# Turning the input by DMA and projecting it as float16 pieces, in an attention and expert kernel

## The reference

```
q  = (xn @ Wq.T + bq) * D**-0.5        # 256 columns: 16 heads of D = 16
kv = xn @ Wkv.T + bkv                  # 32 columns: one key and one value head for all 16
a  = softmax(q_heads @ k.T) @ v        # per batch 16*512 query rows against 512 keys
attn = a @ Wo.T + bo
logits = xn @ w_gate                   # 6 experts, the best one is taken
attn_e = softmax(xn @ tokens_e.T / 16) # 100 tokens for each expert, of rank 16
delta  = ((attn_e @ val_e + xn) @ wd.T + wd_b) * scale
out = x + attn + xn + log(exp(delta of the chosen expert))
```

## Time and profile before

| | |
|---|---|
| median of 3 runs | 976.48 us (974.66 to 976.85) |
| span of the profiled execution | 972.5 us; the median of the runs is 3.98 us above this span, the time around it |
| PE busy | 907.7 us, 93% of the span |
| DVE busy | 808.2 us, 83% |
| ACT busy | 682.1 us, 70% |
| POOL busy | 459.1 us, 47% |
| DMA engines | 29.9% on the one hardware queue |
| mean granted PE clock | 0.981 |

### The profile page before, as it was taken

One profiled execution on the slowest core, in us unless ns is written; L12 is line 12 of the kernel. 1 busy time (PEld: TensorE's weight loads), 2 busy tenths in 40 slices (PEclk: granted clock), 3 DMA queues, 4 the chain that ended last, 5 costly groups with the idle time before them and its releaser, 6 DMA issues.

```text
span 972.5 us, 17720 instructions
## 1 busy us (share of the span) xinstructions
PE 907.7 (93%) x5868; PEld 354.1 (36%) x5868; DVE 808.2 (83%) x1556; ACT 682.1 (70%) x1380; POOL 459.1 (47%) x567
## 2 busy tenths in 40 slices
PE   4889999999999999999999999999999999998976
PEld 3433333333434333343334333333333334332323
DVE  5688978889898888989888898989889898888814
ACT  1217777877777777777777777777777777777791
POOL 3654545554554555455444655444465544524200
PEclk9779999999999999999999999999999999999998
DMA  4230232422324242422423242242423223241120
GB/s 118 70 59 31 76 67 71 91 87 81 91 72 100 63 98 79 95 76 83 88 84 79 89 91 69 91 82 93 88 71 91 81 76 84 71 90 46 58 66 33
DMA packets 86192, 76.07 MB, mean 78 GB/s; under 512 B 18263, under 2 KB 70232, under 8 KB 86104
## 3 DMA queue, kind: packets, MB, share of 16 engines
q1 hardware_dynamic: 86104, 74.94, 29.9%
HBM read 39.28 MB, written 33.54 MB: 75 GB/s over the span
## 4 chain that ended last, share of the span: by engine, by line
PE 75%; DVE 6%; DMA 6%; ACT 6%; POOL 3%; issue 2%; SPq 2%; POOLq 0%; DVEq 0%
PE pO L349 22%; PE pA L331 14%; PE pB L336 8%; PE pA L470 6%; PE pA L412 6%; PE pA L488 5%; DVE M L750 3%; DMA o_parts<-OTr 3%; ACT P L597 3%; PE pA L472 3%; PE pA L402 3%; PE pB L392 2%; SPq L937 2%; PE pA L443 2%; DMA Rb<-l_parts 2%
## 5 line engine op out<-in xcount | busy, mean ns | idle before, releaser
L750 DVE TENSOR_REDUCE M<-pA 128x1 f32<-128x512 f32 x1024 | 652.4, 680 | 82.7 <-PE pA L331 80.9
L597 ACT ACTIVATE P<-pB 128x512 f32<-128x512 f32 x1002 | 553.5, 599 | 147.6 <-PE pB L336 143.1
L331 PE MATMUL pA<-K,Q 48*128 48x512 f16 x1024 | 316.8, 387 | 19.9 <-DVE M L750 10.3
L336 PE MATMUL pB<-Q,K 50*128 50x512 f16 x1002 | 307.3, 383 | 0.3 <-ACT P L597 0.3
L349 PE MATMUL pO<-P,VK 128*32 128x512 f32 x2048 | 272.8, 605 | 11.1 <-ACT P L597 7.9
L331 PEld LDWEIGHTS pA<-K,Q 48*128 48x128 f16 x1024 | 64.0, 94 | 323.2 <-DVE M L750 243.8
L887 POOL TENSOR_TENSOR On<-Op,Rb 128x512 f32<-128x512 f32 x31 | 39.9, 1288 | 146.9 <-DMA Rb<-l_parts 104.7
L873 POOL TENSOR_SCALAR Cz<-Cx 128x512 f32<-128x512 f32 x32 | 62.0, 1936 | 50.4 <-ACT Cx L579 50.4
L349 PEld LDWEIGHTS pO<-P,VK 128*32 128x32 f32 x2048 | 40.4, 108 | 108.3 <-issue 82.2
L412 PE MATMUL pA<-xT,wq 128*128 128x256 f32 x256 | 74.1, 416 | 1.3 <-ACT xT L541 0.7
L488 PE MATMUL pA<-wo,On 128*128 128x256 f32 x248 | 69.9, 407 | 4.3 <-DVE RL L763 2.5
(11 more groups left out here) (130 smaller groups left out, 865.7 us busy)
## 6 DMA issues: line engine op xcount, KB each, us to landing
o_parts<-OTr SPq DMA_DIRECT2D x62, 256.0 KB, 2.3
Q<-q_pieces SPq DMA_DIRECT2D x90, 128.0 KB, 4.1
X<-in_x SPq DMA_DIRECT2D x16, 512.0 KB, 3.9
q_pieces<-Qp SPq DMA_DIRECT2D x32, 256.0 KB, 2.1
out<-OUT SPq DMA_DIRECT2D x32, 256.0 KB, 3.1
Op<-o_parts SPq DMA_DIRECT2D x31, 256.0 KB
Rb<-l_parts SPq DMA_DIRECT2D x31, 256.0 KB
K<-KS SPq DMA_DIRECT2D x96, 16.0 KB, 1.8
```

The costliest lines, as they stand in the source:

```text
L331: e.matmul(bank1("ab", t)[:, :], Q16[r:r + 48, b % 2, h, 128 * s:128 * s + 128], K16[r:r + 48, b % 3, :], start=True, stop=True).then_inc( ...
L336: e.matmul(bankB(t)[:, :], K16[r:r + 50, b % 3, 128 * i:128 * i + 128], Q16[r:r + 50, b % 2, :, 32 * hh:32 * hh + 32], start=True, stop=Tr ...
L597: e.activation(P[:, u % PR, :], bankB(u + LB)[:, :], ACT.Exp, scale=alpha).then_inc(S("e"))
L750: e.tensor_reduce(M[:, t // 32 % 2, t % 2, t % 32 // 2:t % 32 // 2 + 1], bank1("ab", t)[:, :], AX, ALU.max, negate=True).then_inc(S("mx"))
```

## The change

`XN` is now scaled by 2^10 and split into two float16 pieces `XP` (`pieces`: POOL a cast and a subtraction; for batch 0 ACT and DVE do it in two halves). SP turns both pieces by one DMA transpose per batch (`xtd`; two for batch 0) into `xT`, now float16. The weights are scaled and split once at the start (`wqP`, `wcP`), and each projection is three float16 products (`PIECES`), over 512 tokens at a time for q and uk, with the scale taken out where the result is evicted. The mask is turned by a DMA transpose too (`mkd`). `Rs` starts from `X` alone (four `tensor_scalar` of 256 columns in place of one `tensor_tensor` of 1024), so `XN` needs one buffer. Slots move.

```diff
+PIECES = ((0, 0), (0, 1), (1, 0))
+XS = 2.0 ** 10
 SLOT = {
-    "root": -91.4, "refine": -90.2, "norm": -87.2, "xt0": -73.1, "xte0": -72.4, "xt1": -69.1, "xte1": -68.4,
-    "residual": 2.3, "q00": -57, "qe00": -56.4, "q01": -53, "qe01": -52.4, "qs0": -51.2, "qw0": -48.2,
+    "root": -91.4, "refine": -90.2, "norm": -87.2, "pieces": -84.2, "xtd": -74.2,
+    "residual": 2.3, "q0": -57, "qe0": -55.4, "qs0": -53.8, "qw0": -50.2, "uk": -53, "uke": -51.4, "ks": -50.2,
...
-                for c in range(2):
-                    if (b := due(f"xt{c}", n)) is not None:
...
-                            mm = e.transpose(bank2(f"xt{c}", b)[:, 128 * i:128 * i + 128],
-                                             XN[:, b % 2, i, 128 * c:128 * c + 128], idf[:, :])
...
+                for g in range(2):
+                    if (b := due(f"q{g}", n)) is not None:
+                        w.wait_ge(*before1(f"q{g}", b))
+                        w.wait_ge(S(f"xt_{b % 2}"), turned(b))
+                        w.wait_ge(S("wqp"), 2)
+                        for k, (wp, xp) in enumerate(PIECES):
+                            for c in range(2):
+                                mm = e.matmul(bank1(f"q{g}", b)[:, :], wqP[:, wp, c, 128 * g:128 * g + 128],
+                                              xT[:, b % 2, :, xp, c, :], start=(k == 0 and c == 0), stop=(k == 2 and c == 1))
                         mm.then_inc(S(f"q{g}"))
...
-                        for c in range(2):
-                            e.matmul(dst, xT[:, b % 2, c, 128 * t:128 * t + 128], wc[:, c, 0:C],
-                                     start=(c == 0), stop=False)
+                        for k, (wp, xp) in enumerate(PIECES):
+                            for c in range(2):
+                                e.matmul(dst, xT[:, b % 2, t, xp, c, :], wcP[:, wp, c, 0:C],
+                                         start=(k == 0 and c == 0), stop=False)
...
-                    o = bank2("mk", b)[:, :].bitcast(BF16)
-                    for i in range(4):
-                        mm = e.transpose(o[0:ER, 128 * i:128 * i + 128], mk[:, i, :], idb[:, :])
...
+                if (b := due("pieces", n)):
+                    w.wait_ge(S("xn"), 4 * b + 4)
+                    w.wait_ge(S(f"xt_{(b - 1) % 2}"), turned(b - 1))
+                    e.tensor_copy(XP[:, :, 0, :], XN[:, :, :]).then_inc(S("xh"))
+                    w.wait_ge(S("xh"), b)
+                    e.tensor_tensor(XP[:, :, 1, :], XN[:, :, :], XP[:, :, 0, :], ALU.subtract).then_inc(S("xl"))
...
                 if (b := due("utm", n)) is not None:
-                    w.wait_ge(S("mke"), b + 1)
+                    w.wait_ge(S("mkd"), 16 * (b + 1))
...
+                if (b := due("xtd", n)) is not None:
+                    w.wait_ge(S("d"), 4 * (b - 1))
+                    if b:
+                        w.wait_ge(S("xl"), b)
+                    for i0, i1 in ((0, 2), (2, 4)) if b == 0 else ((0, 4),):
+                        if b == 0:
+                            w.wait_ge(S("xl0"), i1 // 2)
+                        e.dma_start_transpose(xT[:, b % 2, i0:i1].rearrange("p i k c t -> p (i k c) t"),
+                                              XP[:, i0:i1].rearrange("p i k n -> p (i k n)")).then_inc(S(f"xt_{b % 2}"), 16)
+
+                if (b := due("mkd", n)) is not None:
+                    w.wait_ge(S("mk"), b + 1)
+                    w.wait_ge(S("mk1"), 1)
+                    w.wait_ge(S("mm"), b)
+                    w.wait_ge(S("utm"), b)
+                    e.dma_start_transpose(mkT[:, :].rearrange("p (i t) -> p i t", t=128),
+                                          mk[:, :, :].rearrange("p i n -> p (i n)")).then_inc(S("mkd"), 16)
```

More of the change, by code:

```diff
@@ L306, in before2, with turned @@
             return FREED2[TURNS[1][k][1]](TURNS[1][k][2]) if k >= 0 else (S("id"), 0)
+        def turned(b):
+            return 16 * (b // 2 + 1) + 16 * (b % 2 == 0)
         block = ctx.enter_context(nc.Block())
@@ L362, in _ @@
                     w.wait_ge(*before1("bs", 0))
-                    w.wait_ge(S("ones"), 5)
+                    w.wait_ge(S("ones"), 4)
                     w.wait_ge(S("two"), 1)
-                    e.matmul(bank1("bs", 0)[:, 0:3], one[:, :], fac[:, 0:3], start=True, stop=True).then_inc(S("bs"))
+                    e.matmul(bank1("bs", 0)[:, 0:7], one[:, :], fac[:, 0:7], start=True, stop=True).then_inc(S("bs"))
                 for h in range(2):
@@ L396, in _ @@
-                for k in range(2):
-                    if (b := due(f"uk{k}", n)) is not None:
-                        w.wait_ge(*before1(f"uk{k}", b))
-                        w.wait_ge(S("xte"), 2 * b + 2)
-                        w.wait_ge(S("wcs"), 1)
-                        for c in range(2):
-                            mm = e.matmul(bank1(f"uk{k}", b)[0:UKW, 0:C], wc[:, c, U0:U0 + UKW],
-                                          xT[:, b % 2, c, C * k:C * k + C], start=(c == 0), stop=(c == 1))
-                        mm.then_inc(S("uk"))
@@ L417, in _ @@
                     w.wait_ge(*before2("vg", b))
-                    w.wait_ge(S("xte"), 2 * b + 2)
-                    for c in range(2):
-                        for i in range(4):
-                            mm = e.matmul(bank2("vg", b)[32 * i:32 * i + 32, 0:128], wc[:, c, V0:V0 + 32],
-                                          xT[:, b % 2, c, 128 * i:128 * i + 128], start=(c == 0), stop=(c == 1))
+                    w.wait_ge(S(f"xt_{b % 2}"), turned(b))
+                    w.wait_ge(S("wcp"), 2)
+                    for k, (wp, xp) in enumerate(PIECES):
+                        for c in range(2):
+                            for i in range(4):
+                                mm = e.matmul(bank2("vg", b)[32 * i:32 * i + 32, 0:128], wcP[:, wp, c, V0:V0 + 32],
+                                              xT[:, b % 2, i, xp, c, :], start=(k == 0 and c == 0), stop=(k == 2 and c == 1))
                     mm.then_inc(S("vg"))
@@ L534, in _ @@
                     w.wait_ge(S("w2"), 1)
-                    e.copy(W2[0:ER + 1, :], bank2("w2", 0)[0:ER + 1, 0:C]).then_inc(S("w2e"))
-                for c in range(2):
-                    if (b := due(f"xte{c}", n)) is not None:
-                        w.wait_ge(S("xt"), 2 * b + c + 1)
-                        w.wait_ge(S("d"), 4 * (b - 1))
-                        e.copy(xT[:, b % 2, c, :], bank2(f"xt{c}", b)[:, :]).then_inc(S("xte"))
+                    e.copy(W2r[0:ER + 1, :], bank2("w2", 0)[0:ER + 1, 0:C]).then_inc(S("w2e"))
+                if due("pieces", n) == 0:
+                    for k in range(2):
+                        w.wait_ge(S("xn"), 2 * k + 2)
+                        e.copy(XP[:, 2 * k:2 * k + 2, 0, :], XN[:, 2 * k:2 * k + 2, :]).then_inc(S("xh0"))
                 if (b := due("vge", n)) is not None:
```

242 lines of the change are left out of this document (139 added, 103 removed), and 9 rows, old and new, of tables (FIRST, SLOT).

## The result

The changed kernel takes 1033.97 us (median of 4 runs, 1025.77 to 1037.82) against 975.57 (973.08 to 976.85) for the kernel before on the same chip: ratio 1.0591, 95% interval 1.0541 to 1.0641. The forecast was 949 with a range of 924 to 972, so the result lies outside the range and has the wrong sign. The profiled run has a span of 1036.0 us.

What follows compares the result with a forecast made beforehand. TensorE was taken to set the pace: -3.85 us of work and +0.9 of waiting per batch gave -42.5 over 14.4 batches; with -1 in the last batch and +16 at the start, 949 us, range 924 to 972.

Steps and rivals of the forecast that it cites:

- TensorE's work, -3.85 per batch: TensorE per batch: input transposes -1.2, mask -0.7, q -1.2, uk -0.6, vg +0.45, d -0.6; sum -3.85 us.
- +0.45: TensorE's vg block, 24 instructions at 0.036 us each plus its own starting cost: 0.45 us more per batch.
- a head: Fixed cost of a TensorE block that doesn't follow another block, taken as 0.20 us.
- What comes late: Step on new waits: one expected, TensorE at `mt` for the maxima from GpSimd, +0.9 us per batch, between 0 and 2.0.
- `mt` at +0.9: TensorE waits at `mt` for maxima because GpSimd's `radd0`, about 1.3 us, now precedes them: +0.9 us per batch.
- On doesn't come sooner: GpSimd's `On`: K writes precede the reads leading to it instead of standing between them, so no earlier start.
- Transposes: DMA transposes land in 3.9 us (input) and 2.3 us (mask); the input's costs nothing in steady state up to 14 us.
- The rival's "about 1,215": Slow-transposes rival, chance 0.09: q waits for the turned input; at the upper bound of 29 us landing, about 1,215 us.
- The estimate of 21 us: Input's DMA transpose: if its 16 blocks added up at 1,309 ns each, 21 us, beyond the 14 us of cover.
- Start, +16: Program start: first score matmul 10.5 us late, batch 1's q block at 57 against 40.82, so +16 us; bounds +9 to +24.
- VectorE as the bound: Rival, chance 0.10: VectorE's clumped work sets a period of 54.4 us, only -1.4 per batch; 971 us in all.
- Weight loads: Rival, chance 0.05: TensorE's float16 weight loads show, 3.8 us per batch, eating all the gain; 990 us.

Runs made afterwards that it cites:

- e13: Changed kernel, buffers aligned by padding, K writes behind the broadcast read, reciprocal 2 ticks later, input's transpose behind that read, mask's transpose first: 945.25 us, ratio 0.9712.
- e14: Kernel of e13 without the third product of q (4 matmuls of 512 columns per batch fewer): 932.26 us, ratio 0.9581.
- e10: Kernel before with the reciprocal 2 ticks later; K writes still between the reciprocals' write and the broadcast read: 975.00 us, ratio 1.0005.
- e17: Kernel before with the order of e13 (K writes behind the broadcast read, reciprocal 2 ticks later): 969.47 us, ratio 0.9946.
- e5: Changed kernel with buffers aligned by padding, and the six K writes moved behind the broadcast read: 965.96 us, ratio 0.9894.
- e6: Changed kernel with buffers aligned by padding, reciprocal 2 ticks later and the input's transpose issued behind the broadcast read: 962.96 us, ratio 0.9882.
- e16: Changed kernel, not aligned, with only the six K writes moved behind the broadcast read: 1010.43 us, ratio 1.0365.

## Why the prediction was wrong, point by point

- **TensorE's work, -3.85 per batch: right in kind, its terms too small.** q 1.40 and uk 1.43 in place of 1.52; vg 0.52 where 0.86 and a head were taken, so its +0.45 was nothing; a d block 0.76 with its head where 0.86 was taken. At the measured prices the terms are -1.2 for the transposes, -0.7 for the mask, -1.4, -0.7, -0.1 and -1.1 for q, uk, vg and d: -5.2. TensorE's busy time per batch fell by 3.3 only, from 54.1 to 50.8 us in e13, and e13's period by 3.0. Some 2 us a batch of what the blocks gave don't show in the time; 0.6 of it is the stand behind uk, the rest isn't traced. e14 shows that TensorE's time in q counts in full once it is the bound.
- **What comes late: the step that failed.** It named one wait, `mt` at +0.9, and put the reciprocal at nothing: -3.85 + 0.9 = -2.95 per batch was forecast, +2.8 was measured. The waits of the kernel before already had VectorE there 18 times for 36.3 us, 23.7 of it in the course of the program. Taking 20 us of them away gained that kernel nothing in e10 and 5 us in e17, for TensorE was behind anyway. With less TensorE work per batch that cover shrinks, and the waits themselves grew at once: 3.5 us in one half, 1.5 in the other, 65.7 in all, ahead of maxima that TensorE needs. That they, and not the new work, hold the kernel is shown by e5, e6 and e13; how much of it is lost cover and how much the longer waits isn't separated.
- **"On doesn't come sooner: the K writes now go out before the reads that lead to it [...] with the same total."** The total was the same for GpSimd, but not for VectorE, whose reciprocal stands between those reads. K ahead of the read of the sums costs the short waits; K between reciprocal and broadcast costs the wait at `mt`; K behind both costs neither (e5, e16, e13). The wait at `mt` didn't come in the changed kernel (under 1 us in all).
- **Q's landing: not in the sum at all.** Three tiles of 16 or 32 bytes are in the diff, and what they shift was not looked at. In the order of the change it is worth 39 us of the 58, the largest single step; in the order of e13 it is worth 17.
- **Transposes: right.** 4.6 and 2.7 us for 3.9 and 2.3; no steady wait of q for `xT`. (The rival's "about 1,215" adds up to 1,220 by its own terms.) The estimate of 21 us from the Trainium skill (VectorE: DVE Perf Modes, The three transpose paths), by adding its 1,309 ns for each 128x128 block, is refuted for blocks moved by one instruction: 16 of them land in 4.6 us. What was judged too lightly is SP's time to issue one, 2.9 us in the median, which stood between the reciprocals' write and the broadcast read; e6 moved it away together with the reciprocal, so its own price isn't separated.
- **Start, +16: right in kind, short by 4.5.** 13.4 and 20.5 us where 10.5 and 16 were forecast. The mask's transpose behind the Q reads was seen; putting it ahead gives 2 us. The last wait was another than forecast: batch 1's q block came late behind `En` and the blocks that need it, at the lower clock, and not for its turned input, which had landed at 59.9.
- **The clock: in no term.** The sum was worked out at full speed. The stalls brought TensorE to the lower level for up to 32 us worth of work more than before (estimated above), nearly all of it gone in e13.
- **VectorE as the bound: no**, as e14 shows, apart from the one short stand a batch. **Weight loads: no**, q and d take their pitch.

The accounting, each step a pair of runs: 1034 changed; 995 aligned (-39); 966 with K behind (-29); 945 with the reciprocal later, the transpose behind the broadcast and the mask first (-21). What a step is worth depends on what was done before it: the -29 and -21 together are 50, while on the aligned kernel K alone gave 29 and the reciprocal with the transpose 32. The forecast of 949 and 52.9 us per batch is met by e13 at 945.3 and 52.8. The sum was that of a kernel whose order leaves no new wait, and the changed kernel isn't that one. Nor is e13's number a vindication but luck: the wait of 0.9 at `mt` isn't there, the work taken away was 5.2 in place of 3.85, and with both the period would have been 50.6.

What stays open: whether the write of the heads lands late for the Q reads right ahead of it (they stand there in every case, and faster reads shorten it from 5.0 to 3.8 us, but no run had them well apart, since the buffer comes free too late), when a stall brings the clock down and when it doesn't, what keeps e13's period 2 us above the sum of its terms, and by which mechanism the misplaced destination slows the reads.

## What to carry to other kernels

When work leaves the bounding engine, go through the list of waits of *all* engines for the ones that were free until now, and ask of each how many us of cover remain; 24 us of such waits were worth at most 5 us to the kernel before, and grown to 66 us, with the lower clock behind them, they ate the whole gain and more. When a queue is reordered, write out who stands between each pair of dependent transfers, not the sum over the queue: one place of six small DMAs was worth 33 us in one order and 51 in another. And look at where every buffer of small DMA rows comes to lie after a new tile is declared.

## What the runs showed that I had not expected

- A destination 96 bytes past a multiple of 512 makes reads in pieces of 512 bytes land in 5.0 to 5.1 us in place of 4.1 (medians; over all runs here 5.0 to 5.4 and 4.1 to 4.4), and costs 17 to 39 us in this kernel, by how much room its order leaves.
- One DMA transpose of 512 KB between SBUF tiles holds SP's queue for 2.9 us in the median (1.70 for batch 1's, at the start; 1.25 for the 128 KB one), more than the six Q reads (2.79).
- After a pause of about 2 us TensorE ran 7.6 us at a granted clock of 0.50; after a like one of 2.63 us it didn't. The changed kernel has the lower clock in 44 of 390 slices of 2 us, e13 in 9.
- GpSimd's pieces of the input, as one 128x1024 cast and one subtraction, take 1.04 and 2.13 us.
